# Attention of a two-batch block: score chunks taken ahead of the projection in the heavy steps, and the rest of the step re-ordered to match

## The chip, the cores and the metric

The kernel runs on one core of a Trainium2 chip. The metric is the device time of one execution in microseconds (us), the lower the better. All engines of the core (TensorE or PE, VectorE or DVE, ScalarE or ACT, GpSimd or POOL, and SyncE or SP, which issues all DMAs) run their own instruction lists in order and meet only at semaphores.

## The reference

For 2 batches of 1024 tokens with 512 features it computes `x + s * g`, where `s` is causal attention with ALiBi bias on the layer-normalised input, and `g` the SiLU of a gated feed-forward network.

```python
x = L0_attn_x                       # (2, 1024, 512)
xn = layernorm(x)
q = rmsnorm((xn @ Wq.T) by 32 heads of 128);  k = rmsnorm((xn @ Wk.T) by 8 heads);  v = (xn @ Wv.T) by 8 heads
scores = q @ k.T / sqrt(128) + slope * (key - query)       # -1e30 above the diagonal
s = (softmax(scores) @ v) @ Wo.T
g = silu((silu(xn @ w_gate.T) * (xn @ w_up.T)) @ w_down.T) # inner size 1376
out = x + s * g
```

## The kernel before

Every fp32 operand of a matmul is split in a high half (fp32r) and the rest, and each product is three matmuls (high by high, high by low, low by high). So each tensor that goes to PE is first copied by ACT (`high_...`), and the rest is then made by DVE (`low_...`) or POOL.

The work of a batch is 8 *units*, one for each key/value head with its 4 query heads, and behind them the feed-forward part. A unit is 8 *steps*, one for each tile of 128 queries. Step `i` of unit `U` works on several tiles at once, each engine by a list written out by hand:

- `project` (PE, L365 and L366): q, k and v of tile `i+2`, 24 matmuls. `squares` (ACT) sums their squares, POOL's `norms` makes the reciprocal roots, `scale_qk` (DVE, L751) scales.
- `turn_qk` (PE, L374): transposes of tile `i+1`, then `high_q`, `high_k` (ACT) and `low_q`, `low_k` (DVE, L757, L763). `project` of a tile writes the PSUM accumulator of the tile two before, and so waits until `low_q` and `low_k` of that one are done (`qk_low`).
- `out_project` (PE, L414): the attention output of tile `i-3` by `w_o`, once DVE has scaled it (`scale_att`, L811) and split it (`low_att`, L818). `add_y` (DVE, L827) then empties the PSUM bank `out_ps`.
- `scores` (PE, L388): 4 heads by 1 or 2 *chunks*; tiles 0 to 3 have 1 chunk a head (4 in all), tiles 4 to 7 have 2 (8 in all, up to 512 wide). Chunks go round three PSUM banks, so a chunk waits until DVE's `bias` (L780, which adds the bias, tracks the row minimum and moves the chunk to `probs`) has emptied the bank of three chunks ago.
- `exp` (ACT, L563) of each head, `turn_blocks` (DVE, L791), 32x32 transposes inside the tile, then 16 DMAs issued by SP (`turn_probs`, L273) that bring the blocks home into `pT_lo`, transposed.
- `weigh` (PE, L402): for the tile `p = i-2`, `p+1` blocks of probabilities by v into `out_ps`. Each block needs `high_probs` (ACT, L571) and `low_probs` (DVE, L803); there are four slots for the high halves. The first block also waits for `add_y`.

In step 0 `weigh` works on tile 6 of the unit before, in step 1 on tile 7. In steps 2 to 4 (`LANDS_LATE`) the halves stand later in the lists, since the DMAs land late there. In step 5 ACT and POOL also split the next unit's weights (`high_w`, `low_w`), and in step 2 those of `w_o` (`high_o`, 1.0 us for each of two parts).

PE's list of a step before is `project`, `turn_qk`, `out_project`, all `scores`, `weigh`. What is called a heavy step below is one of 5, 6 and 7.

## Time and profile before

| | us |
|---|---|
| median of 3 runs (lowest, highest) | 2480.33 (2474.41, 2491.34) |
| the profiled execution | 2487.69 |
| its span, first to last instruction | 2485.8 |
| from the start to the end of batch 0's attention, with the start-up | 1028 |
| batch 0's feed-forward part | 236 |

The profiled execution is 7.4 us above the median; 1.9 us of its time lie around the span. The second batch repeats the first. Within a batch the six units between the first and the last are alike; one of them, from 1803.10 to 1929.41 us (its steps 2 to 7 and steps 0 and 1 of the one that follows), is the one that the rows further down look at.

### The profile page before, as it was taken

What the parts mean: (1) busy time and instruction counts of PE and PEld (TensorE: products, weight loads), DVE (VectorE), ACT (ScalarE), POOL (GpSimd) and SP (SyncE); (2) the same over time, 40 slices, a digit from 0 to 9 for tenths busy, and PEclk for the clock granted to TensorE, in tenths of its full rate; (3) what the DMA queues carried; (4) which work ended last, traced back from release to release, by engine and by line L of the source; (5) the groups of instructions that cost most, each with busy time, mean ns of one, the idle gap of its engine ahead of it and who ended that gap; (6) DMA issues with size and microseconds to landing.
All of it is one profiled execution on the core that took longest, in us unless ns stands there. A gap on an engine that the chain in (4) does not pass through costs nothing.

```text
span 2485.8 us, 36949 instructions
## 1 busy us (share of the span) xinstructions
PE 2278.6 (92%) x10928; PEld 1858.0 (75%) x10928; DVE 1794.6 (72%) x3788; ACT 1330.2 (54%) x3700; POOL 826.0 (33%) x2053
## 2 busy tenths in 40 slices
PE   6899989999999999799988999999999999997998
PEld 5777777777777777678877777777777777776887
DVE  5788778787878796831458888888888887887132
ACT  3556555555556565543345565656565556554333
POOL 1424233333332323234514141424242424240443
PEclk8999999999999999999999999999999999999999
DMA  2576857485768585753317766676657766748223
GB/s 91 110 119 97 133 90 135 91 125 103 121 109 119 106 118 102 134 115 124 135 43 129 127 105 107 117 118 114 106 122 102 125 104 114 117 81 158 90 96 108
DMA packets 432681, 277.08 MB, mean 111 GB/s; under 512 B 104672, under 2 KB 399712, under 8 KB 428512
## 3 DMA queue, kind: packets, MB, share of 16 engines
q1 hardware_dynamic: 432480, 274.72, 59.6%
q8 instruction: 87, 1.43, 0.4%
q14 instruction: 114, 0.93, 0.3%
HBM read 119.12 MB, written 4.46 MB: 50 GB/s over the span
## 4 chain that ended last, share of the span: by engine, by line
PE 52%; DVE 20%; issue 7%; SPq 7%; POOL 5%; ACT 4%; DMA 3%; ACTq 0%; DVEq 0%; POOLq 0%
PE out_ps L414 11%; DVE probs L780 9%; PE out_ps L402 9%; SPq L273 7%; PE even_ps L365 5%; PE score_ps L475 5%; PE qkv_ps L365 4%; PE qkv_ps L475 4%; POOL qkv_lo L1032 4%; DVE pT_lo L803 3%; DVE probs L791 3%; PE even_ps L366 3%; PE even_ps L491 2%; PE qkv_ps L366 2%; DMA pT_lo<-probs 2%
## 5 line engine op out<-in xcount | busy, mean ns | idle before, releaser
L563 ACT ACTIVATE probs<-probs,low_min 128x896 f32<-128x896 f32 (+7 forms) x512 | 396.0, 777 | 318.4 <-DVE low_min L780 314.5
L803 DVE TENSOR_TENSOR pT_lo<-pT_lo,pT_hi 128x512 fp32r<-128x512 f32 x576 | 379.0, 693 | 72.3 <-ACT pT_hi L571 71.9
L791 DVE STREAM_TRANSPOSE probs<-probs 128x896 f32<-128x896 f32 (+7 forms) x512 | 382.5, 760 | 0.4
L1002 POOL TENSOR_SCALAR rs_x<-sq_sum 128x5 f32<-128x5 f32 x122 | 24.7, 203 | 1031.2 <-ACT natural L539 1020.6
L571 ACT ACTIVATE pT_hi<-pT_lo 128x512 fp32r<-128x512 f32 x576 | 326.6, 625 | 66.0 <-DMA pT_lo<-probs 47.3
L402 PE MATMUL out_ps<-pT_hi,kv_hi 128*128 128x512 f32 x576 | 247.2, 429 | 97.0 <-DVE pT_lo L803 91.6
L576 ACT ACTIVATE attT_hi<-att 128x512 fp32r<-128x512 f32 x128 | 80.9, 632 | 325.1 <-DVE att L811 325.1
L402 PEld LDWEIGHTS out_ps<-pT_hi,kv_hi 128*128 128x128 f32 x576 | 110.9, 193 | 169.6 <-DVE pT_lo L803 107.9
L402 PE MATMUL out_ps<-pT_lo,kv_hi 128*128 128x512 f32 x576 | 231.5, 402 | 0.0
L402 PE MATMUL out_ps<-pT_hi,kv_lo 128*128 128x512 f32 x576 | 231.2, 401 | 0.0
L388 PE MATMUL score_ps<-kv_hi,qT_hi 128*128 128x384 f32 (+5 forms) x512 | 189.6, 370 | 44.6 <-DVE low_min L780 38.8
L414 PE MATMUL out_ps<-o_hi,attT_hi 128*128 128x512 f32 x512 | 214.0, 418 | 10.7 <-DVE attT_lo L818 10.7
L780 DVE CUSTOM_DVE_ANT_0 probs<-score_ps,rel_sb,slope 128x384 f32<-128x384 f32 (+5 forms) x352 | 202.2, 581 | 6.2 <-DMA pT_lo<-probs 2.4
L414 PE MATMUL out_ps<-o_hi,attT_lo 128*128 128x512 f32 x512 | 203.3, 397 | 0.0
L414 PE MATMUL out_ps<-o_lo,attT_hi 128*128 128x512 f32 x512 | 201.9, 394 | 0.0
L1032 POOL TENSOR_TENSOR qkv_lo<-qkv_raw,qkv_hi 128x768 fp32r<-128x768 f32 x63 | 115.0, 1847 | 194.1 <-ACT qkv_hi L586 181.7
L388 PE MATMUL score_ps<-kv_hi,qT_lo 128*128 128x384 f32 (+5 forms) x512 | 175.4, 342 | 0.0
L388 PE MATMUL score_ps<-kv_lo,qT_hi 128*128 128x384 f32 (+5 forms) x512 | 175.1, 342 | 0.0
L827 DVE TENSOR_TENSOR y<-out_ps,y 128x512 f32<-128x512 f32 x118 | 81.5, 691 | 127.2 <-PE out_ps L414 125.7
L388 PEld LDWEIGHTS score_ps<-kv_hi,qT_hi 128*128 128x128 f32 x512 | 96.8, 189 | 93.6 <-DVE low_min L780 75.1
L1051 POOL TENSOR_TENSOR kv_lo<-qkv_raw,kv_hi 128x1024 fp32r<-128x1024 f32 x44 | 106.4, 2418 | 123.9 <-ACT kv_hi L608 123.9
L402 PEld LDWEIGHTS out_ps<-pT_hi,kv_lo 128*128 128x128 f32 x576 | 111.7, 194 | 25.6
(201 smaller groups left out, 6165.6 us busy)
## 6 DMA issues: line engine op xcount, KB each, us to landing
qkv_raw<-w_ffn_dram SPq DMA_DIRECT2D x44, 768.0 KB, 4.3
att<-rec_out_at SPq DMA_DIRECT2D x128, 256.0 KB
pT_lo<-probs SPq DMA_DIRECT2D x256, 128.0 KB
pT_lo<-probs SPq DMA_DIRECT2D x256, 112.0 KB
pT_lo<-probs SPq DMA_DIRECT2D x256, 96.0 KB
qkv_raw<-w_qkv_dram SPq DMA_DIRECT2D x15, 1536.0 KB
pT_lo<-probs SPq DMA_DIRECT2D x256, 80.0 KB
o_raw<-w_o_dram SPq DMA_DIRECT2D x16, 1024.0 KB, 7.6
```

Source lines behind the costliest of these rows:

```text
L273: sp.dma_start(homes[b * SQUARE:(b + 1) * SQUARE, :, a], by_chunk[i % 2][a * SQUARE:(a + 1) * SQUARE, 0:i + 1, b]).then_inc(probs_back[t % ...
L365: pe.matmul(acc[:, 0:BANK], a, w[:, c, 0:D], start=go, stop=end)
L388: mm = pe.matmul(score_all[n % SBANKS][:, 0:hi - lo], q[:, i % 2, h * P:(h + 1) * P], kt[:, lo:hi], start=(q is qT_hi and kt is kT_hi), st ...
L402: mm = pe.matmul(out_ps[:, :], v[:, j * P:(j + 1) * P], pt, start=(j == 0 and v is v_hi and pt is high), stop=(j == i and v is v_lo))
L414: mm = pe.matmul(out_ps[:, :], a[:, h * P:(h + 1) * P], w[:, h * D:(h + 1) * D], start=(h == 0 and a is attT_hi and w is o_hi), stop=(h == ...
L475: mm = pe.matmul(acc, w[slot][:, at:at + P], xT[:, d, half * BANK:(half + 1) * BANK], start=(d == 0 and w is gu_hi and xT is xT_hi), stop= ...
L563: act.activation(row, row, ACT.Exp, scale=-1.0, bias=low_min[:, i % 2, h, HEAD_CHUNKS[i] - 1:HEAD_CHUNKS[i]], accum_out=row_sum[:, i % 2, ...
L571: act.activation(pT_hi[:, n % HIGH_SLOTS, :], home(i, j).bitcast(F32), ACT.Copy).then_inc(probs_high, 1)
L780: dve.tensor_tensor_reduce(out=by_head[i % 2][:, h, lo // SQUARE:hi // SQUARE, :], in0=score_all[n % SBANKS][:, 0:hi - lo].rearrange("p (m ...
L791: dve.transpose(row, row).then_inc(probs_turned, 1)
L803: dve.tensor_tensor(out=home(i, j), in0=home(i, j).bitcast(F32), in1=pT_hi[:, n % HIGH_SLOTS, :].bitcast(F32), op=ALU.subtract).then_inc(p ...
L1032: pool.tensor_tensor(out=qkv_lo[:, c, :], in0=qkv_raw[:, c, :], in1=qkv_hi[:, c, :].bitcast(F32), op=ALU.subtract).then_inc(w_split if U e ...
```

## The change

A function `parts_of` says how many chunks of a step PE makes ahead of `project` and how many between `project` and `turn_qk`. In the first unit of a batch it says none. In steps 0 to 4 of the other units three stand between `project` and `turn_qk`, and the rest behind `out_project`; in steps 5 to 7 three stand ahead of `project`, three between it and `turn_qk`, and two behind `out_project`. DVE's biases and ACT's exponentials follow this: in heavy steps DVE makes the first three biases ahead of its first four `low_probs`, three more behind them, and the transpose of head 0 ahead of `low_q`; ACT makes head 0's exponential ahead of `squares`, and `high_q`, `high_k` behind `stage_v`. The remaining `low_probs` of a heavy step stand right behind the last bias, ahead of the transposes of heads 1 to 3, and not between them. `low_k` of the next unit's tile 0 (step 7) moves from behind the last bias to behind the transposes of heads 1 and 2. In step 2 `high_o` moves from ahead of `high_probs` to behind three exponentials. In step 5 two of the four `high_w` stand ahead of `high_q`, two behind it.

The rest changes nothing that runs: the slot of a high half is now counted through all units (36 turns in a unit are a multiple of the 4 slots, so that the numbers are the same), `stats` lies in `att[1]`, and the scratch for dynamic DMAs is 256 bytes and not 1024.

```diff
+        def parts_of(i, first):
+            chunks = G * HEAD_CHUNKS[i] if i < TILES else 0
+            if first or not chunks:
+                return 0, 0, chunks
+            return (SBANKS, 2 * SBANKS, chunks) if i > HT else (0, SBANKS, chunks)
...
             def step(U, i, first, last):            # PE
+                ahead, between, chunks = parts_of(i, first)
+                for k in range(ahead):
+                    scores(U, i, k, first)
                 if not (last and i >= TILES - 2):
                     project(U + (i + 2) // TILES, (i + 2) % TILES, first and i + 2 < TILES)
+                for k in range(ahead, between):
+                    scores(U, i, k, first)
                 if not (last and i >= TILES - 1):
                     turn_qk(U + (i + 1) // TILES, (i + 1) % TILES, first and i + 1 < TILES)
...
-                for k in range(sooner):
-                    scores(U, i, k, first)
                 if not (first and i <= LAG):
                     out_project(U, i)
-                for k in range(sooner, chunks):
+                for k in range(between, chunks):
                     scores(U, i, k, first)
...
+                    for h in heads[:ahead // 2]:    # ACT
+                        exp(U, i, h)
+                    heads = heads[ahead // 2:]
...
+                    for h in heads[:-1]:
+                        exp(U, i, h)
+                    if i == LAG:
+                        high_o(U, 0, not first)
+                        high_o(U, 1, not first)
+                    if ahead:
+                        for j in highs:
                             high_probs(V, p, j)
-                        highs = highs[1:]
-                        exp(U, i, G - 1)
...
+                    for k in range(ahead):          # DVE, behind low_att
+                        bias(U, i, k)
...
+                    for k in range(ahead, between): # behind the first four low_probs
+                        bias(U, i, k)
+                    for h in heads[:ahead // 2]:
+                        turn_blocks(U, i, h)
...
-                    if i == TILES - 1 and not last:
-                        low_k(U + 1, 0, False)
...
+                    if ahead:
+                        for j in lows:
+                            low_probs(V, p, j)
+                        lows = []
+                    for h in heads:
+                        for j in lows[:1]:
+                            low_probs(V, p, j)
+                        lows = lows[1:]
+                        if h == G - 1:
+                            if i == TILES - 1 and not last:
+                                low_k(U + 1, 0, False)
+                            reciprocals(U, i)
+                        turn_blocks(U, i, h)
...
-    nc = bacc.Bacc("TRN2", target_bir_lowering=False, num_devices=1, dynamic_dma_scratch_size=1024)
+    nc = bacc.Bacc("TRN2", target_bir_lowering=False, num_devices=1, dynamic_dma_scratch_size=256)
```

**The head of step 7.** On PE, in the fourth unit, the list before from the last matmul of `weigh` (L402) on:

```order
L402 MATMUL out_ps<-pT_hi,kv_lo 128x512
L365 MATMUL qkv_ps<-qkv_hi,xT_hi 128x512
L366 MATMUL qkv_ps<-qkv_hi,xT_hi 128x256
L365 MATMUL qkv_ps<-qkv_lo,xT_hi 128x512
L366 MATMUL qkv_ps<-qkv_lo,xT_hi 128x256
L365 MATMUL qkv_ps<-qkv_hi,xT_lo 128x512
L366 MATMUL qkv_ps<-qkv_hi,xT_lo 128x256
```

and now (L410 is `weigh`, L396 `scores`, L373 and L374 are `project`):

```order
L410 MATMUL out_ps<-pT_hi,kv_lo 128x512
L396 MATMUL score_ps<-kv_hi,qT_hi 128x512
L396 MATMUL score_ps<-kv_lo,qT_hi 128x512
L396 MATMUL score_ps<-kv_hi,qT_lo 128x512
L396 MATMUL third_ps<-kv_hi,qT_hi 128x512
L396 MATMUL third_ps<-kv_lo,qT_hi 128x512
L396 MATMUL third_ps<-kv_hi,qT_lo 128x512
L396 MATMUL score_ps<-kv_hi,qT_hi 128x512
L396 MATMUL score_ps<-kv_lo,qT_hi 128x512
L396 MATMUL score_ps<-kv_hi,qT_lo 128x512
L373 MATMUL qkv_ps<-qkv_hi,xT_hi 128x512
```

Three chunks have come between the last weighing and the projection. On DVE at the same place, before (L811 `scale_att`, L751 `scale_qk`, L818 `low_att`, L803 `low_probs`, L757 `low_q`, L827 `add_y`, L780 a bias with its read of the minimum):

```order
L811 TENSOR_TENSOR att<-out_ps,att 128x512
L751 TENSOR_TENSOR natural<-even_ps,rq 128x640
L818 TENSOR_TENSOR attT_lo<-att,attT_hi 128x512
L803 TENSOR_TENSOR pT_lo<-pT_lo,pT_hi 128x512 x4
L757 TENSOR_TENSOR qT_lo<-even_ps,qT_hi 128x512
L827 TENSOR_TENSOR y<-out_ps,y 128x512
L780 ISA probs,low_min<-score_ps,rel_sb,slope 128x16x32
L780 ISA low_min 128x1
```

and now (the same functions are L837, L777, L844, L829, L783, L853 and L806):

```order
L837 TENSOR_TENSOR att<-out_ps,att 128x512
L777 TENSOR_TENSOR natural<-even_ps,rq 128x640
L844 TENSOR_TENSOR attT_lo<-att,attT_hi 128x512
L806 ISA probs,low_min<-score_ps,rel_sb,slope 128x16x32
L806 ISA low_min 128x1
L806 ISA probs,low_min<-third_ps,rel_sb,low_min,slope 128x16x32
L806 ISA low_min 128x1
L806 ISA probs,low_min<-score_ps,rel_sb,slope 128x16x32
L806 ISA low_min 128x1
L829 TENSOR_TENSOR pT_lo<-pT_lo,pT_hi 128x512 x4
L806 ISA probs,low_min<-score_ps,rel_sb,low_min,slope 128x16x32
L806 ISA low_min 128x1
```

Three biases stand ahead of the four `low_probs`, and `low_q` and `add_y` come later than these rows.

**The end of step 7 on DVE,** from the last bias on, before (L791 `turn_blocks`, L763 `low_k` of the next unit's tile 0, L798 `reciprocals`):

```order
L780 ISA probs,low_min<-third_ps,rel_sb,low_min,slope 128x16x32
L780 ISA low_min 128x1
L791 STREAM_TRANSPOSE probs<-probs 128x32x32
L763 SCALAR_TENSOR_TENSOR kv_lo<-even_ps,wcol,kv_hi 128x128
L803 TENSOR_TENSOR pT_lo<-pT_lo,pT_hi 128x512
L791 STREAM_TRANSPOSE probs<-probs 128x32x32
L803 TENSOR_TENSOR pT_lo<-pT_lo,pT_hi 128x512
L798 RECIPROCAL rec<-row_sum 128x4
L791 STREAM_TRANSPOSE probs<-probs 128x32x32
```

and now (L817, L789 and L824):

```order
L806 ISA probs,low_min<-third_ps,rel_sb,low_min,slope 128x16x32
L806 ISA low_min 128x1
L829 TENSOR_TENSOR pT_lo<-pT_lo,pT_hi 128x512 x2
L817 STREAM_TRANSPOSE probs<-probs 128x32x32 x2
L789 SCALAR_TENSOR_TENSOR kv_lo<-even_ps,wcol,kv_hi 128x128
L824 RECIPROCAL rec<-row_sum 128x4
L817 STREAM_TRANSPOSE probs<-probs 128x32x32
```

Both `low_probs` have moved ahead of all three transposes, and `low_k` from ahead of two of them to behind two.

**Step 2 on ACT,** from `high_att` (L576) on, before (L550 `high_q`, L556 `high_k`, L539 `squares`, L546 `stage_v`, L583 `high_o`, L571 `high_probs`, L563 `exp`):

```order
L576 ACTIVATE attT_hi<-att 128x512
L550 ACTIVATE qT_hi<-qkv_ps 128x512
L556 ACTIVATE kv_hi<-qkv_ps,wcol 128x128
L539 ACTIVATE natural,sq_sum<-even_ps 128x128 x5
L546 ACTIVATE v_nat<-even_ps 128x128
L583 ACTIVATE o_hi<-o_raw 128x1024 x2
L571 ACTIVATE pT_hi<-pT_lo 128x512
L563 ACTIVATE probs,row_sum<-probs,low_min 128x12x32 x4
```

and now (L585, L548, L555, L559, L565, L580, L572 and L592):

```order
L585 ACTIVATE attT_hi<-att 128x512
L548 ACTIVATE natural,sq_sum<-even_ps 128x128 x5
L555 ACTIVATE v_nat<-even_ps 128x128
L559 ACTIVATE qT_hi<-qkv_ps 128x512
L565 ACTIVATE kv_hi<-qkv_ps,wcol 128x128
L580 ACTIVATE pT_hi<-pT_lo 128x512
L572 ACTIVATE probs,row_sum<-probs,low_min 128x12x32 x3
L592 ACTIVATE o_hi<-o_raw 128x1024 x2
L572 ACTIVATE probs,row_sum<-probs,low_min 128x12x32
```

The one `high_probs` of this step no longer stands behind `high_o`.

## Rows read from the trace of the kernel before

**Rows 1.** The page: busy us of each engine, share of the span, instructions.

```profile
PE 2278.6 (92%) x10928; PEld 1858.0 (75%) x10928; DVE 1794.6 (72%) x3788; ACT 1330.2 (54%) x3700; POOL 826.0 (33%) x2053
```

**Rows 2.** Steps 5, 6, 7, 0, 1, 2, 3, 4, then all: us; busy PE, PEld, DVE, ACT, POOL (instructions); clock; DMA.

```profile
1843.23:1858.19 14.96, 14.96 (x78) 12.68 (x77) 14.43 (x32) 11.96 (x31) 5.68 (x13) 1.00 0.71 121
1858.19:1877.03 18.84, 16.93 (x82) 13.37 (x80) 18.13 (x34) 10.56 (x29) 8.80 (x22) 1.00 0.78 161
1877.03:1898.55 21.52, 19.14 (x85) 14.80 (x83) 19.10 (x36) 11.04 (x28) 3.23 (x15) 0.92 0.77 98
1898.55:1914.14 15.59, 15.49 (x75) 12.99 (x74) 10.18 (x26) 8.36 (x29) 3.72 (x15) 0.89 1.09 136
1914.14:1929.41 15.27, 15.13 (x79) 12.27 (x78) 11.89 (x27) 9.31 (x30) 3.22 (x15) 1.00 0.22 49
1803.10:1815.11 12.01, 10.62 (x58) 9.05 (x57) 6.48 (x14) 7.02 (x22) 3.99 (x14) 1.00 0.45 144
1815.11:1827.80 12.69, 12.15 (x61) 9.70 (x60) 10.07 (x23) 7.40 (x26) 8.92 (x19) 1.00 0.32 73
1827.80:1843.23 15.43, 14.28 (x75) 11.66 (x74) 12.84 (x33) 8.21 (x26) 4.59 (x15) 1.00 0.39 89
1803.10:1929.41 126.31, 118.70 (x582) 96.53 (x581) 103.12 (x220) 73.84 (x218) 42.16 (x126) 0.97 0.62 110
```

**Rows 3.** The waits of PE: in total, times, longest.

```profile
PE out_ps L402 <- DVE pT_lo L803: 91.6, 89, 2.6
```

**Rows 4.** DVE in order of time, steps 5 to 7: start, us, what, [idle before].

```profile
1845.27 0.65 DVE L811 TENSOR_TENSOR att<-out_ps,att 128x512 f32<-128x512 f32 x1
...
1867.18 0.69 DVE L827 TENSOR_TENSOR y<-out_ps,y 128x512 f32<-128x512 f32 x1 [0.54 <-PE out_ps L414]
...
1884.70 0.69 DVE L827 TENSOR_TENSOR y<-out_ps,y 128x512 f32<-128x512 f32 x1 [1.49 <-PE out_ps L414]
1885.49 0.75 DVE L780 CUSTOM_DVE_ANT_0 probs<-score_ps,rel_sb,slope 128x512 f32<-128x512 f32 x1
...
1890.08 1.24 DVE L791 STREAM_TRANSPOSE probs<-probs 128x1024 f32<-128x1024 f32 x1
...
1898.79 0.69 DVE L811 TENSOR_TENSOR att<-out_ps,att 128x512 f32<-128x512 f32 x1 [0.52 <-PE out_ps L402]
```

**Rows 5.** PE in order of time, step 7 and the start of step 0.

```profile
1877.03 0.40 PE L365 MATMUL qkv_ps<-qkv_hi,xT_hi 128*128 128x512 f32 x1
...
1884.50 0.39 PE L388 MATMUL score_ps<-kv_hi,qT_hi 128*128 128x512 f32 x1
1884.73 0.39 PE L388 MATMUL score_ps<-kv_lo,qT_hi 128*128 128x512 f32 x1
...
1895.38 0.79 PE L402 MATMUL out_ps<-pT_hi,kv_hi 128*128 128x512 f32 x1 [2.29 <-DVE pT_lo L803]
...
1898.55 0.63 PE L365 MATMUL even_ps<-qkv_hi,xT_hi 128*128 128x512 f32 x1
```

**Rows 6.** The window of 4 us at the end of step 7 (columns as in rows 2).

```profile
1896.00:1900.00 4.00, 3.92 (x11) 2.73 (x10) 3.48 (x6) 0.48 (x1) 0.00 (x0) 0.50 0.06 1
```

**Rows 7.** PE in order of time, end of step 2: first block weighed.

```profile
1814.34 0.47 PE L402 MATMUL out_ps<-pT_hi,kv_hi 128*128 128x512 f32 x1 [1.39 <-DVE pT_lo L803]
```

**Rows 8.** SP issues the 16 DMAs of tile 7, in two units: start, us until all are issued.

```profile
925.71 14.02 SPq L273 DMA_DIRECT2D pT_lo<-probs  x16
...
1898.85 12.95 SPq L273 DMA_DIRECT2D pT_lo<-probs  x16
```

**Rows 9.** ACT takes tile 7's first blocks, in the same two units.

```profile
947.08 2.19 ACT L571 ACTIVATE pT_hi<-pT_lo 128x512 fp32r<-128x512 f32 x4 [6.27 <-DMA pT_lo<-probs]
...
1916.07 2.20 ACT L571 ACTIVATE pT_hi<-pT_lo 128x512 fp32r<-128x512 f32 x4 [0.37 <-DMA pT_lo<-probs]
```

**Rows 10.** Step 1 of the first of these two units (columns as in rows 2).

```profile
939.26:959.71 20.45, 16.27 (x79) 13.57 (x77) 11.97 (x27) 9.63 (x30) 3.66 (x15) 0.92 0.50 138
```

**Rows 11.** The DMA queue of nearly all bytes: packets, MB, share of 16 engines.

```profile
q1 hardware_dynamic: 432480, 274.72, 59.6%
```

82 lines of the change are left out of this document (40 added, 42 removed).

## The prediction

> **What bounds the kernel now.** I read the page first [rows 1]: PE is busy for 2278.6 us, 92% of the span, and DVE for 1794.6. Matmuls overlap in these records (0.39 us each, while the next starts 0.23 us later [rows 5]), so busy time says little of what PE could save. What counts is how long a step lasts against PE's own work in it. The table by steps [rows 2] shows the steady unit: 126.31 us for eight steps. PE's work in a step: projection, turn and output projection take 7.47 us together (1877.03 to 1884.50 [rows 5]); each 512 columns of scores or weighing take 0.23 us, three times a chunk or block, narrower chunks in proportion. That gives, for steps 5, 6, 7: 7.47 + 8 x 0.52 + 4 x 0.69 = 14.4; 7.47 + 8 x 0.60 + 5 x 0.69 = 15.7; 7.47 + 8 x 0.69 + 6 x 0.69 = 17.1. They last 14.96, 18.84 and 21.52. So some 8 us of a unit are lost in these steps. DVE's busy time in steps 6 and 7 is 18.13 of 18.84 and 19.10 of 21.52 [rows 2]: there DVE sets the pace, not PE, and PE's longest wait in total is for `low_probs` (91.6 us in 89 waits [rows 3]).
>
> DVE in order of time [rows 4] shows why DVE itself isn't full. `add_y` waits for PE, which has projection and output projection ahead of it: 1.49 us in step 7, 0.54 in step 6. Only behind it may the biases start (1885.49, 8.5 us into the step), and all eight come in one run with the transposes. So the last two `low_probs` are late, PE idles for 2.29 us before the fifth block [rows 5], and DVE then waits 0.52 us for PE. PE's clock falls with it: the granted clock is 0.50 in the last window, the lower of its two levels (1.2 GHz), and 0.92 and 0.89 over steps 7 and 0 [rows 2, 6].
>
> **The heavy steps.** The change removes no instruction and adds none; it gives DVE three biases at the head of the step, while PE projects. From `scale_att` of step 5 to that of step 0 DVE takes 1898.79 - 1845.27 = 53.52 us, of which three waits are 0.54 + 1.49 + 0.52 = 2.55 [rows 4]: 51.0 of work and small gaps. A bias of 512 costs 0.77 (1885.49 to 1890.08 for six [rows 4]), so in step 7 DVE does `scale_att`, `scale_qk`, `low_att` (2 us), three biases (2.3), four `low_probs` (2.4), and is at 8.4 us when PE has made chunks 3 to 5 (2.1 + 4.2 + 2.1 = 8.4). Three biases and a transpose more and it is at 11.9, `low_q` 12.5, and PE has ended the output projection at 11.6. So `add_y` no longer waits for PE; PE waits for it, until 13.1 (0.3 us after its last chunk). The last two biases end at 14.6, both `low_probs` at 15.8, before PE comes to blocks 5 and 6 at 15.9. PE ends the step at 17.3 and the 2.29 us are gone.
>
> What is late next is `low_k` of the next unit's tile 0. The projection of step 0 writes the accumulator that it reads, so PE waits for it. In DVE's list it now stands behind two more transposes of 1.24 us [rows 4]: 15.8 + 2.3 + 0.3 = 18.4. That is a new wait of 1.1 us in each unit, with PE's whole next projection queued behind it. DVE still has the reciprocals and one transpose to do, 1.3 us.
>
> So steps 5 to 7 last as long as DVE's work: it enters step 5 some 1.6 us behind PE (2.0 before, 1845.27 against the step's start), works 51.0, and releases PE 1.3 before its end: 1.6 + 51.0 - 1.3 = 51.3, against 55.32 before. **Gain 4.0.** Bounds: nothing, if other waits take the place of the three; 7 if DVE's small gaps close too and its backlog is pushed on into step 0, which has room (10.18 busy of 15.59 [rows 2]). The weight split of step 5 (`high_w`, then POOL) starts 1.5 us later with the projection, but the next projection starts 1.8 us later too: no change.
>
> **The clock.** Without the idle PE at the end of step 7 the granted clock should stay at 1.00; step 0 would be 0.89 x 15.59 = 13.9. I take 14.1, **gain 1.5.** The Trainium skill (TensorE: Matmul & The Clock Gate, What's actually happening) says that the low clock is the default and activity lifts it, and so any idle stretch could bring the fall. By that rule the wait for `low_k` may keep the fall, and some 18 us of the total with it; the row shows the fall only behind the 2.29 us wait.
>
> **Step 1 loses.** Tile 7's blocks come home by 16 DMAs that SP issues once all is transposed. The issue takes 13 to 14 us [rows 8], and ACT's first copy came 1916.07 - 1898.85 = 17.2 us after the first issue [rows 8, 9], in step 1. Now the last transpose ends 1.3 us into step 0, the issue starts 0.6 later, and the blocks are there at 1.9 + 17.2 = 19.1, which is 5.0 us into step 1 (1.9 before). ACT's list has `squares`, `high_q` and all exponentials behind that copy. In the unit where the blocks came 7.8 us into step 1 (947.08 against 939.26) ACT sat idle for 6.27 us and the step lasted 20.45 [rows 9, 10], 12.6 us beyond the landing. The three biases now stand in front of `low_q` and chunks are made earlier, which I put at 0.6 us less: 5.0 + 12.0 = 17.0 against 15.27. **Loss 1.7**; bounds: no loss if the DMAs are quicker in a less dense stretch, 6 if all land as late as in that unit (21.4 us after the issue).
>
> **The light steps.** In step 2 PE waits 1.39 us before its only block [rows 7], because ACT's `high_probs` stands behind two `high_o` of 1.0 us each; now it is ahead of them. What stands behind `high_o` is POOL's `low_o` and, behind that, `out_project` of step 3; its second half ends later by about as much as `high_o` does, 0.5 us by my placing of the exponentials, and three chunks now stand in front of `out_project`, 2 us, so it should still be in time. **Gain 1.3** (0 to 1.4). Step 3: PE's work is 7.47 + 4 x 0.69 + 2 x 0.69 = 11.6 of 12.69. Three biases done before `add_y` leave one behind it, and both low halves are ready: **gain 0.9** (0 to 1.1). Step 4: work 7.47 + 8 x 0.44 + 3 x 0.69 = 13.1 of 15.43; the five biases behind `add_y` still pace PE, **gain 1.4** (0 to 2.3). All of these move DVE's work into stretches where it idled; behind them stands only DVE's lag of some 2 us at a step's start, which the projection hides.
>
> **The sum.** 4.0 + 1.5 - 1.7 + 1.3 + 0.9 + 1.4 = 7.4 us in a steady unit. There are 12: 89 us. The two last units have the light steps' gain and the output projection's wait of step 7 hidden by chunks made ahead, but are bound by DVE in steps 6 and 7: 5 us each. The two first have no chunks ahead; their low halves stand in front of the transposes: 2 us each. Together 103 us. The feed-forward part doesn't change. The profiled execution of 2487.69 would take 2385; it lies 7.4 above the median, so 2377, and I say 2375.
>
> **The rivals.**
> - DMA lateness eats more (0.20). If tile 7 lands 21.4 us after the issue in each unit, step 1 lasts 4.2 us more: gain 3.2 a unit, 12 x 3.2 + 14 = 52, 2428. For it: SP's issue and the DMA engines are already dense in step 0 (share 1.09 [rows 2]), and steps get shorter while SP's work of a tile stays at 13 us or more. Against: one unit alone shows it.
> - The heavy steps gain nothing (0.08): the waits for `low_k`, for `add_y` behind `low_q`, and for slots of high halves eat the 4.0. Then 3.4 a unit, 2425.
> - More than forecast (0.17): DVE's small gaps close, step 1 isn't late: 10.5 a unit in all 14 units that change, 147 us, 2333. PE's own work would still allow it.
> - Slower (0.02): the issue of the DMAs gets slower with the scratch cut to a quarter. SP needs about 1.7 us around the 16 DMAs of each of 8 tiles; at 12.95/16 = 0.81 us a DMA [rows 8] that is 8 x 14.6 = 117 us a unit. From 0.90 us a DMA SP alone would pace a unit at 128.8 and the kernel would be over 1% slower; at 1.0 us it is 142 a unit, 2480 + 14 x 15.3 = 2694. Against: the queue is `hardware_dynamic` [rows 11]. The Trainium skill (DMA: Bandwidth & Descriptors, SWDGE vs HWDGE vs iDMA) says that the ring in SBUF serves DMAs issued from GpSimd, and that those from SP have none; by that rule the cut costs nothing, and no run here shows it yet.
> - No difference (0.03): every place that gains is paid back by SP's pace, 14.6 a tile with stalls a little longer than now, 0.88 us a DMA: 2470.
>
> **How the numbers follow.** The forecast has 0.50, with its own range 2350 to 2405. The range of 8 in 10 takes in a good part of the larger gain and of the DMA rival: 2330 to 2430. A measurement of this kernel can tell 1%, 25 us, from no change. Faster by more: 0.50 + 0.20 + 0.08 + 0.17 = 0.95; same 0.03; slower 0.02.
>
> **What would show it.** In the changed profile a steady unit should last about 119 us; step 7 about 18.4, with a wait of the first projection matmul of step 0 for `low_k` of some 1 us in place of the 2.29 us before the fifth block; the granted clock at 1.00 there; ACT's first copy in step 1 waiting some 3 to 4 us for the DMA in most units; no wait in step 2. Wrong would be: `add_y` still waiting for PE in heavy steps; step 1 under 16 us; SP's issue longer than 14 us for a tile.

## The result, and the profile after

The changed kernel takes **2419.7 us** (median of 4 runs, 2408.71 to 2429.22) against 2482.76 us for the kernel before in the same job (4 runs). The ratio is 0.9744, with a 95% interval of 0.969 to 0.9799. The profiled execution takes 2429.22 us, its span is 2427.3, so it is 58.5 us under the span of 2485.8 before. It is the slowest of the four runs: the numbers of waits and steps below are of one execution, and another of the same kernel can differ, as after_again shows further down.

The page's busy time of each engine, to be held against [rows 1]; behind it the page's chain of work that ended last, by engine:

```profile
PE 2231.9 (92%) x10928; PEld 1859.3 (77%) x10928; DVE 1797.2 (74%) x3788; ACT 1332.8 (55%) x3700; POOL 812.3 (33%) x2053
PE 50%; SPq 19%; DVE 10%; issue 8%; DMA 5%; POOL 4%; ACT 4%; ACTq 0%; DVEq 0%; POOLq 0%
```

The instructions are the same in number. DVE had 20% of the chain before and SP's queue 7%; now DVE has 10% and SP's queue 19%. The change took much of DVE's work off the path, and what came onto it is the issue of DMAs.

The table by steps shows where: steps 5, 6, 7, 0, 1, 2, 3, 4 and their sum, of the stretch of the second batch that begins nearest to the one of [rows 2] (columns as there):

```profile
1804.66:1820.39 15.73, 14.68 (x79) 12.84 (x77) 15.41 (x34) 11.71 (x31) 5.39 (x11) 1.00 0.81 117
1820.39:1836.65 16.26, 16.17 (x81) 13.68 (x80) 15.74 (x33) 9.98 (x27) 9.21 (x24) 1.00 1.13 177
1836.65:1855.51 18.86, 17.49 (x85) 14.05 (x83) 18.48 (x36) 11.04 (x28) 3.52 (x15) 1.00 0.96 132
1855.51:1870.01 14.50, 13.95 (x75) 11.92 (x76) 11.02 (x28) 8.58 (x29) 3.23 (x15) 1.00 0.71 100
1870.01:1888.25 18.24, 16.45 (x79) 13.49 (x77) 11.79 (x27) 9.61 (x30) 3.28 (x15) 0.91 0.41 89
1888.25:1899.15 10.90, 10.59 (x57) 9.07 (x56) 6.90 (x16) 6.64 (x23) 3.25 (x14) 1.00 0.53 168
1899.15:1911.12 11.97, 11.82 (x60) 9.69 (x59) 11.41 (x23) 8.32 (x27) 9.59 (x19) 1.00 0.49 79
1911.12:1925.11 13.99, 13.39 (x75) 11.68 (x74) 12.29 (x31) 8.14 (x26) 4.54 (x15) 1.00 0.71 98
1804.66:1925.11 120.45, 114.54 (x581) 96.41 (x580) 103.04 (x221) 74.02 (x219) 42.00 (x126) 0.99 0.74 120
```

Every step but 1 and 5 is shorter, DVE's busy time is the same (103.04 and 103.12), and the granted clock no longer falls in steps 7 and 0; it falls in step 1 (0.91), which is 3 us longer. The units aren't alike any more. So the numbers below are means over the 12 steady units of a trace; a step is measured from the start of its first matmul to that of the next step's.

| mean of 12 units, us | 0 | 1 | 2 | 3 | 4 | 5 | 6 | 7 | unit |
|---|---|---|---|---|---|---|---|---|---|
| before | 15.44 | 15.56 | 11.99 | 12.69 | 15.46 | 15.17 | 18.93 | 21.36 | 126.59 |
| changed | 14.62 | 17.40 | 10.82 | 12.25 | 15.31 | 15.58 | 16.64 | 19.21 | 121.83 |
| least of the 12, changed | 14.48 | 15.62 | 10.79 | 11.97 | 13.99 | 14.44 | 16.16 | 18.83 | |

The wait of 2.29 us before the fifth block [rows 5] is gone, and a wait of the next projection for `low_k` stands in its place: first PE at the start of step 0 and DVE's `low_k`, then the window of 4 us ahead of it, to be held against [rows 6] (two views of the changed kernel).

```profile
1855.51 0.50 PE L373 MATMUL even_ps<-qkv_hi,xT_hi 128*128 128x512 f32 x1 [1.30 <-DVE kv_lo L789]
...
1855.14 0.31 DVE L789 SCALAR_TENSOR_TENSOR kv_lo<-even_ps,wcol,kv_hi 128x128 fp32r<-128x128 f32 x1
```

```profile
1852.00:1856.00 4.00, 2.69 (x13) 1.95 (x12) 4.00 (x7) 1.60 (x4) 0.00 (x0) 1.00 0.48 114
```

The largest waits of the changed kernel that matter here, from the list of waits (us in total, times, longest):

```profile
ACT pT_hi L580 <- DMA pT_lo<-probs: 80.0, 34, 7.1
...
DVE probs L806 <- DMA pT_lo<-probs: 43.0, 23, 4.7
...
DVE y L853 <- PE out_ps L422: 38.9, 33, 3.4
...
PE even_ps L373 <- DVE kv_lo L789: 18.7, 14, 1.6
...
PE out_ps L410 <- DVE pT_lo L829: 6.3, 6, 1.4
```

PE's wait for `low_probs` fell from 91.6 us [rows 3] to 6.3, and the wait for `low_k` gives back 18.7, 1.3 in each of 14 units. The first two lines are the 16 DMAs of a tile. ACT's `high_probs` waited for them before too, for 47.3 us in 23 waits. The second line is new in this size: before it was 4.2 us in 3 waits; now 27.9 of its 43.0 us lie in step 4. It is `bias`, which may not write `probs` before the DMAs of the tile *two before* have read it, since two `probs` buffers take turns. In step 4 of one unit (DVE and SP in order of time, changed kernel):

```profile
2032.43 0.69 DVE L844 TENSOR_TENSOR attT_lo<-att,attT_hi 128x512 fp32r<-128x512 f32 x1
2036.02 0.55 DVE L806 CUSTOM_DVE_ANT_0 probs<-score_ps,rel_sb,slope 128x320 f32<-128x320 f32 x1 [2.90 <-DMA pT_lo<-probs]
...
2006.96 14.60 SPq L281 DMA_DIRECT2D pT_lo<-probs  x16
2022.93 10.23 SPq L281 DMA_DIRECT2D pT_lo<-probs  x16
```

SP needed 14.60 us for the 16 DMAs of tile 1, so that the 16 of tile 2 were issued by 2033.16 only; the wait for them ended at 2036.0. The first bias of tile 4, which the change had put at the head of the list, waited 2.90 us for them, with `low_q`, `low_k` and all other biases behind it. This step 4 lasted 16.71 us, where the one in the table above lasted 13.99.

### The profile page after: what moved, and what is told of

It is laid out like the page before. It is cut to its first block, busy times and chain, and to the rows that moved or that the text cites. A ratio compares the mean times of both kernels' runs of the same rounds, so it can differ in the third digit from the quotient of the medians.

```text
span 2427.3 us, 36949 instructions
## 1 busy us (share of the span) xinstructions
PE 2231.9 (92%) x10928; PEld 1859.3 (77%) x10928; DVE 1797.2 (74%) x3788; ACT 1332.8 (55%) x3700; POOL 812.3 (33%) x2053
## 4 chain that ended last, share of the span: by engine, by line
PE 50%; SPq 19%; DVE 10%; issue 8%; DMA 5%; POOL 4%; ACT 4%; ACTq 0%; DVEq 0%; POOLq 0%
SPq L281 17%; PE out_ps L410 9%; PE out_ps L422 7%; PE score_ps L396 5%; PE score_ps L484 5%; PE qkv_ps L484 5%; PE qkv_ps L373 3%; PE even_ps L373 3%; DMA pT_lo<-probs 3%; DVE probs L817 3%; DVE probs L806 2%; PE third_ps L396 2%; PE even_ps L500 2%; DVE pT_lo L829 2%; POOL qkv_lo L1067 2%
## 5 line engine op out<-in xcount | busy, mean ns | idle before, releaser
L572 ACT ACTIVATE probs<-probs,low_min 128x896 f32<-128x896 f32 (+7 forms) x512 | 395.6, 784 | 145.7 <-DVE low_min L806 142.5
L829 DVE TENSOR_TENSOR pT_lo<-pT_lo,pT_hi 128x512 fp32r<-128x512 f32 x576 | 374.4, 689 | 135.1 <-ACT pT_hi L580 133.5
L580 ACT ACTIVATE pT_hi<-pT_lo 128x512 fp32r<-128x512 f32 x576 | 331.1, 624 | 179.5 <-PE out_ps L410 93.5
L817 DVE STREAM_TRANSPOSE probs<-probs 128x896 f32<-128x896 f32 (+7 forms) x512 | 372.3, 754 | 0.0
L410 PE MATMUL out_ps<-pT_hi,kv_hi 128*128 128x512 f32 x576 | 243.0, 422 | 66.1 <-issue 46.7
L585 ACT ACTIVATE attT_hi<-att 128x512 fp32r<-128x512 f32 x128 | 81.0, 633 | 346.8 <-DVE att L837 345.5
L806 DVE CUSTOM_DVE_ANT_0 probs<-score_ps,rel_sb,slope 128x384 f32<-128x384 f32 (+5 forms) x352 | 204.3, 591 | 51.5 <-DMA pT_lo<-probs 41.7
L396 PE MATMUL score_ps<-kv_hi,qT_hi 128*128 128x384 f32 (+5 forms) x512 | 180.3, 352 | 60.7 <-DVE low_min L806 57.2
L410 PE MATMUL out_ps<-pT_hi,kv_lo 128*128 128x512 f32 x576 | 231.3, 401 | 0.0
L410 PE MATMUL out_ps<-pT_lo,kv_hi 128*128 128x512 f32 x576 | 231.0, 401 | 0.0
L410 PEld LDWEIGHTS out_ps<-pT_hi,kv_hi 128*128 128x128 f32 x576 | 112.4, 195 | 124.2 <-issue 75.3
L396 PE MATMUL score_ps<-kv_hi,qT_lo 128*128 128x384 f32 (+5 forms) x512 | 175.9, 344 | 0.0
L396 PE MATMUL score_ps<-kv_lo,qT_hi 128*128 128x384 f32 (+5 forms) x512 | 175.6, 343 | 0.0
L396 PEld LDWEIGHTS score_ps<-kv_hi,qT_hi 128*128 128x128 f32 x512 | 97.4, 190 | 88.6 <-DVE low_min L806 72.1
L410 PEld LDWEIGHTS out_ps<-pT_hi,kv_lo 128*128 128x128 f32 x576 | 111.7, 194 | 25.6
L844 DVE TENSOR_TENSOR attT_lo<-att,attT_hi 128x512 fp32r<-128x512 f32 x128 | 124.9, 975 | 5.6 <-ACT attT_hi L585 5.6
```

Of the source, the lines that this page charges most:

```text
L396: mm = pe.matmul(score_all[n % SBANKS][:, 0:hi - lo], q[:, i % 2, h * P:(h + 1) * P], kt[:, lo:hi], start=(q is qT_hi and kt is kT_hi), st ...
L410: mm = pe.matmul(out_ps[:, :], v[:, j * P:(j + 1) * P], pt, start=(j == 0 and v is v_hi and pt is high), stop=(j == i and v is v_lo))
L572: act.activation(row, row, ACT.Exp, scale=-1.0, bias=low_min[:, i % 2, h, HEAD_CHUNKS[i] - 1:HEAD_CHUNKS[i]], accum_out=row_sum[:, i % 2, ...
L580: act.activation(pT_hi[:, (U * TURNS + n) % HIGH_SLOTS, :], home(i, j).bitcast(F32), ACT.Copy).then_inc(probs_high, 1)
L806: dve.tensor_tensor_reduce(out=by_head[i % 2][:, h, lo // SQUARE:hi // SQUARE, :], in0=score_all[n % SBANKS][:, 0:hi - lo].rearrange("p (m ...
L817: dve.transpose(row, row).then_inc(probs_turned, 1)
```

## Experiments

Ratios are against the kernel before on the same chip, with their 95% intervals. The steps are those of one profiled execution of each, and that one can lie off the median: by 9 us in before_half and by 15 in after_again, both below it. The first four ran on one chip (before: 2468.66 us), the next four on another (2472.07), the last four on a third (2472.28). All means of steps are made like those above.

| | us | ratio | unit | step 0 | 1 | 2 | 3 | 4 | 5 to 7 |
|---|---|---|---|---|---|---|---|---|---|
| scratch1024 | 2386.87 | 0.9674 [0.9633, 0.9715] | 118.73 | 14.62 | 16.01 | 10.81 | 12.01 | 14.33 | 50.95 |
| light_only | 2452.18 | 0.9922 [0.989, 0.9954] | 124.22 | 16.04 | 15.57 | 10.83 | 12.13 | 14.66 | 54.99 |
| heavy_only | 2444.39 | 0.9896 [0.9861, 0.9932] | 123.39 | 14.46 | 17.46 | 10.54 | 14.28 | 15.38 | 51.26 |
| low_k_first | 2380.3 | 0.964 [0.9612, 0.9669] | 118.35 | 14.55 | 16.73 | 10.82 | 12.21 | 14.42 | 49.60 |
| after_again | 2392.73 | 0.9665 [0.964, 0.969] | 118.63 | 14.75 | 15.73 | 10.81 | 11.99 | 14.32 | 51.03 |
| scratch_again | 2387.98 | 0.9658 [0.9634, 0.9681] | 119.48 | 14.74 | 16.18 | 10.82 | 12.02 | 14.52 | 51.21 |
| half_issue | 2373.71 | 0.9604 [0.9587, 0.9621] | 118.60 | 14.74 | 15.61 | 10.81 | 12.00 | 14.00 | 51.45 |
| split_issue | 2433.68 | 0.9859 [0.9834, 0.9884] | 121.92 | 16.07 | 15.92 | 10.80 | 12.23 | 14.19 | 52.71 |
| before_half | 2462.47 | 0.9959 [0.9941, 0.9976] | 125.04 | 14.77 | 15.26 | 11.97 | 12.65 | 15.43 | 54.95 |
| half_low_k | 2349.68 | 0.9508 [0.9487, 0.9528] | 116.83 | 14.50 | 15.58 | 10.81 | 12.00 | 14.00 | 49.93 |
| heavy_q_first | 2441.66 | 0.9885 [0.9858, 0.9911] | 123.17 | 14.69 | 16.34 | 10.91 | 14.39 | 16.64 | 50.20 |
| half_blocks | 2380.62 | 0.9629 [0.9605, 0.9652] | 118.95 | 14.77 | 15.61 | 10.82 | 12.15 | 14.63 | 50.98 |

**scratch1024: is it the scratch?** The changed kernel with the scratch of before.

```diff
-dynamic_dma_scratch_size=256
+dynamic_dma_scratch_size=1024
```

> The changed kernel with the scratch for dynamic DMAs back at 1024 bytes, nothing else. Theory A (the scratch serves no DMA of this kernel, and SP's issue is as long as before): as the changed kernel, 2420 us, ratio to before 0.974 within half a per cent, and SP still some 12 us for the 16 DMAs of a tile. Rival B (the smaller scratch slows the issue and is why the DMAs come late): under 2400 us, issue nearer 10.3 us a tile.

It came out well under the changed kernel's result, and under theory B's bound too, but with 11.71 us for the issue of 16 DMAs and not nearer 10.3, and on another chip. So it was run again (scratch_again) beside the changed kernel itself (after_again).

> The changed kernel once more, to stand beside the next three on one chip. Its first comparison gave a ratio to before of 0.9744 [0.969, 0.980] on another chip; with the scratch at 1024 on a later chip the ratio was 0.9674 [0.963, 0.972]. If the scratch is without effect, this one and the next agree within half a per cent.

> The changed kernel with 1024 bytes of scratch, on the same chip as the 256 bytes of the run ahead. Theory A (the scratch does nothing, and chips differ in how fast their DMAs land): the same ratio as the run ahead within 0.5%. Rival B (256 bytes cost something): 0.7% or 17 us less than the run ahead.

Side by side they are 0.9658 and 0.9665, with intervals that overlap: no effect of the scratch is seen. The Trainium skill (DMA: Bandwidth & Descriptors, SWDGE vs HWDGE vs iDMA) gives DMAs issued from SP no ring in SBUF; these two runs agree with it. What the first run had seemed to show is how comparisons differ: the same changed kernel has 0.9744 in the first one and 0.9665 here. The waits tell which part differs between the two traces. Of after_again, the waits for the 16 DMAs:

```profile
ACT pT_hi L580 <- DMA pT_lo<-probs: 30.4, 21, 3.1
...
DVE probs L806 <- DMA pT_lo<-probs: 15.8, 10, 3.3
```

46.2 us instead of 123.0. Step 2 is the same in both and steps 5 to 7 differ by 0.4 us; steps 1 and 4 differ by 1.7 and 1.0 (15.73 and 14.32 against 17.40 and 15.31). But the trace of after_again is of the fastest of its five executions (2377.79, the slowest took 2394.74), the first one of the slowest of four. scratch_again's trace, of an execution of 2394.05 us on the same chip, has 48.9 us of these waits. So part of the difference is between executions on one chip, and how much of it is the chip isn't shown.

**light_only, heavy_only: which part gives what?** `parts_of` alone is changed.

```diff
-            return (SBANKS, 2 * SBANKS, chunks) if i > HT else (0, SBANKS, chunks)
+            return 0, SBANKS, chunks                                                 # light_only
+            return (SBANKS, 2 * SBANKS, chunks) if i > HT else (0, 0, chunks)        # heavy_only
```

> Heavy steps 5 to 7 take three chunks between projection and turn and none ahead of the projection, like the light steps; the rest as changed. Theory A (the heavy steps' chunks ahead are worth 4 us a unit, of which DMA lateness in the steps behind eats some 2): steps 5 to 7 last about 54 to 55 us, step 1 back at 15.3 to 15.6, step 7 again with a wait of PE for the low halves or for add_y: 2440 to 2455 us. Rival C (chunks between projection and turn already feed DVE in time, the ones ahead bring nothing): 2420 us as changed.

> Steps 0 to 4 make no chunk between projection and turn (all four or eight stand behind the output projection, as before); the heavy steps and ACT's and DVE's order as changed. Theory A (light steps gain little in sum, since their early biases only meet the wait for the DMAs that empty the probabilities' buffer, some 1.5 to 2 us a unit come from step 2 alone): 2425 to 2440 us, with hardly a wait of a bias for a DMA in step 4. Rival D (the light steps' chunks are worth the 3.6 us a unit that was forecast for steps 2 to 4): 2460 to 2470 us.

Each alone gives some 1%, both together give 3.3% (scratch1024, same chip). light_only came out as its theory A said; heavy_only is 4 us above its theory A and 16 below rival D. Its other sign of theory A is there: no bias waited for the DMAs at all, so it takes the light steps' early chunks to bring that wait. The steps say why the parts don't add up. Chunks ahead in the heavy steps give 4.2 us in steps 5 to 7 in heavy_only as well (55.46 to 51.26). But in both halves the *lists around the chunks* stay as the change made them, and each has a price if its cover is missing. In light_only `low_k` stands late although no bias of step 7 is ahead of the projection: step 7 lasts 21.83 and the next projection waits for it (19.2 us in 14 waits). The granted clock of the step 0 behind it is 0.87 in one unit (1743.60 to 1759.94), and step 0 lasts 16.04 in the mean. In heavy_only step 3 lasts 14.28 us against 12.69 before, and DVE waits for ACT there.

**heavy_q_first: is it `squares` ahead of `high_q`?** heavy_only, with ACT's order of before in the light steps:

```diff
-                    if first:
+                    if not between:
                         turned()          # high_q, high_k
                     ... squares, stage_v ...
-                    if not first:
+                    if between:
                         turned()
```

> heavy_only (chunks ahead in steps 5 to 7 alone, 2444.39 us on its chip, ratio 0.9896) with one more edit: in steps 0 to 4 ACT makes high_q and high_k ahead of squares and stage_v, as before the change. In heavy_only the steady step 3 takes 14.05 us against 12.69 us before, and DVE waits there for ACT's high_q. Theory A, the two parts of the change help each other since ACT's new order (squares first) needs the chunks between projection and transposes: with high_q first, step 3 is 12.7 us again, step 2 stays under 12.0, and the time falls by 12 x 1.3 = 16 us or somewhat more, to 2425 us, ratio 0.982. Theory B, the order of ACT is nothing, and it is the lateness of the DMAs that makes the sum of the parts less than the whole: step 3 stays near 14 us, 2444 us, ratio 0.990.

No: step 3 stays at 14.39, and 2441.66 us is near theory B's 2444. The order of `high_q` isn't what makes it long; that the lateness of the DMAs does, as theory B went on, isn't seen either, since one wait of a bias for them is left (1.0 us). The list of waits of heavy_q_first and DVE in order of time show another of the moved pieces:

```profile
DVE rec L824 <- ACT probs L572: 22.7, 16, 1.5
```

```profile
1780.34 0.18 DVE L824 RECIPROCAL rec<-row_sum 128x4 f32<-128x4 f32 x1 [1.45 <-ACT probs L572]
```

The last exponential of step 2 now stands behind both `high_o` (1.99 us), and without chunks made ahead DVE has nothing else left and waits 1.45 us for it. heavy_only has the same wait (22.5 us, 16 times); in the changed kernel it is 4.4 us in all. It is of the size of most of the 1.7 us in step 3, but that it is the cause isn't shown: a version with `high_o` alone moved wasn't run. A rival is untested as well. The change also moved the transposes of heads 0 and 1 in the light steps, from between the biases to behind all of them, and this stays in both versions. Where step 4's 16.64 comes from (15.38 in heavy_only) I didn't settle.

**half_issue, before_half: what do the DMAs cost each kernel?** SP issues 8 of the 16 DMAs of a tile; what they would have brought stays zero, so that half of the transposed probabilities are left out. The compute engines do the same work in the same order otherwise, with one more memset by POOL at the start.

```diff
-PER_TURN = BLOCKS * BLOCKS * 16
+PER_TURN = BLOCKS * BLOCKS // 2 * 16
...
-                    for k in range(BLOCKS):
+                    for k in range(BLOCKS // 2):
```

> The changed kernel with 8 of the 16 DMAs that bring a tile's blocks home left out (half of each block's squares stay what they were, so the output is not the reference's), and one memset more at the start. SP's issue and the bytes both halve. Theory A (late DMAs are what the forecast's gain was lost to, 2 to 3 us a unit on average over their floors in steps 1, 3, 4 and 5): no wait of ACT or DVE for these DMAs, steps 1, 3, 4 at their shortest, 15.6, 12.0 and 14.0, unit about 117.5 us, 30 to 50 us below the changed kernel. Rival D (the engines' own order sets the time): at most 10 us below.

> This is the kernel before the change, with 8 of the 16 DMAs of each tile left out (half of the transposed probabilities stay zero, and the waits count 8). It asks what the transfers cost the kernel before, as half_issue (2373.71 us) asked it of the changed one. Theory A, the earlier chunks are what brings the waits for these DMAs to the path: before, only one of the twelve steady units stands above its usual 126.3 us (287.32 to 420.49 us, 133.17 us), so that the transfers cost it some 7 us in all, 2472 - 7 = 2465 us, ratio 0.997. The changed kernel without them would then be 91 us under this one, 7.6 us for each steady unit, and the transfers would account for the rest of what was missing. Theory B, the transfers cost both kernels alike: half_issue was 19 us under the changed kernel on its chip, so 2472 - 19 = 2453 us, ratio 0.992.

The changed kernel gains 19 us on its chip (2392.73 to 2373.71), and no wait of ACT or DVE for these DMAs is left. That is less than the 30 to 50 us of theory A (against the 2419.7 us of the first comparison it would be 46) and more than rival D's 10; steps 1, 3 and 4 are at the lengths theory A named (15.61, 12.00 and 14.00), in all 12 units. The kernel before gains 10 us (2472.28 to 2462.47), near theory A's 7. Between their two traces the unit is 1.55 us shorter, 0.67 of it in step 0. So the kernels differ by 88.8 us without the lateness, by 79 with it on that chip, and by 63 in the first comparison. SP's issue of a tile's 16 takes about as long in both kernels (11.64 us in the mean before, 12.02 and 11.63 in the two traces of the changed one). The kernel before waited for them too, and the changed kernel waits at more places.

**half_blocks: issue or bytes?** All 16 DMAs are issued, each with half of the blocks (again half of the probabilities are left out).

```diff
-    homes[..., :, a],              by_chunk[..., 0:i + 1, b]
+    homes[..., 0:(i + 2) // 2, a], by_chunk[..., 0:(i + 2) // 2, b]
```

> The changed kernel with all 16 DMAs of each tile issued, but each carrying only the first (i+2)/2 of the i+1 blocks, about half the bytes (half of the transposed probabilities stay zero). With half as many DMAs of full size the changed kernel took 2373.71 us, and 2392.73 with all. Theory A, what is late is SP's issue (16 in a row take 11.6 us a tile): it stays late with half the bytes, 2388 us or more. Theory B, it is the bytes in the DMA engines (from the last issue to the landing): 2374 to 2378 us.

2380.62 lies between the two theories, and so does the ratio. Step 1 is as short as in half_issue (15.61), step 4 isn't (14.63). Its waits:

```profile
DVE probs L809 <- DMA pT_lo<-probs: 20.7, 10, 4.5
ACT pT_hi L583 <- DMA pT_lo<-probs: 12.7, 14, 3.2
```

SP's issue of 16 took 11.56 us in the mean of all tiles, and 11.63 in after_again: half the bytes don't shorten the issue. Tile 7 had landed (the last event of its semaphore) 13.0 us after its first issue instead of 16.0, in the mean of its 16 units. So, as far as single executions on two chips can be compared, ACT's wait in step 1 depends on the bytes (1.8 us left of 21.2) and DVE's wait in step 4 on the issue (15.6 us against 13.1). The one follows the largest tile; ahead of the other are two short steps (10.8 and 12.0 us), in which SP, with 10 to 16 us a tile, falls behind.

**split_issue: let ACT issue four of them.** Four of the 16 DMAs of a tile go to ACT's queue, behind `high_att`.

```diff
-                for a in range(BLOCKS):            # SP
+                for a in range(BLOCKS - 1):
...
+                    a = BLOCKS - 1                 # ACT, behind high_att
+                    for k in range(BLOCKS):
+                        act.dma_start(homes[...], by_chunk[...])
```

> The changed kernel with 4 of the 16 DMAs of each tile issued by ACT, behind its copy for the attention output at the head of the next step, and 12 by SP; all that is computed stays. If SP's issue of 16 times 0.65 us is what makes the blocks late (theory A1), they land 2.5 us sooner in the light tiles and most waits of biases for DMAs in steps 3 and 4 go: 10 to 25 us less than the changed kernel. If bytes and engines set the landing (A2), only SP's queue gets shorter: within 5 us. ACT pays 4 issues a step, which delays its high halves by up to 2.5 us: it could cost 10 us and more if ACT's order counts (rival D).

It is worse, by 41 us against after_again, as rival D had it. The lateness did shrink, as theory A1 had it: 13.2 us of ACT's waits for these DMAs are left and none of DVE's, of 46.2. But ACT pays for it. The list of waits, then ACT in order of time at the head of an ordinary step 5:

```profile
ACT pT_hi L580 <- issue: 173.9, 74, 5.5
```

```profile
1800.11 2.58 ACTq L634 DMA_DIRECT2D pT_lo<-probs  x4
1802.79 2.20 ACT L580 ACTIVATE pT_hi<-pT_lo 128x512 fp32r<-128x512 f32 x4 [2.11 <-issue]
```

Four issues hold ACT for 2.62 us as a rule (the median of 128 tiles, from 2.50 up), with `high_probs` behind them and `low_probs` and PE behind those. Against after_again step 0 went from 14.75 to 16.07 in the mean and step 5 from 15.54 to 17.27. The slowest four of all took 5.94 us:

```profile
1851.16 5.94 ACTq L634 DMA_DIRECT2D pT_lo<-probs  x4
1857.20 2.19 ACT L580 ACTIVATE pT_hi<-pT_lo 128x512 fp32r<-128x512 f32 x4 [5.47 <-issue]
```

and the windows of the steps 7 and 0 around it (columns as in rows 2):

```profile
1830.45:1849.33 18.88, 17.52 (x85) 14.05 (x83) 18.50 (x36) 10.81 (x28) 3.23 (x15) 1.00 0.86 112
1849.33:1869.98 20.65, 16.64 (x74) 13.70 (x75) 11.25 (x28) 8.56 (x29) 3.22 (x15) 0.83 0.95 115
```

This step 0 lasted 20.65 us, those of the other steady units 15.4 to 16.4. The Trainium skill (Trainium Kernel Development and Optimization, Key Constraints) says that issuing from several engines only saves the sequencer's issue time. Here that time was what SP lacked. One issue cost ACT as much as SP (0.65 us at 2.62 for four), but on ACT it stood ahead of work that PE waits for.

**low_k_first: the wait for `low_k`.** `low_k` stands ahead of the transposes of step 7, `high_k` ahead of the last exponential.

```diff
                     if i == TILES - 1 and not last:      # ACT
                         high_k(U + 1, 0, False)
                     for h in heads[-1:]:
                         exp(U, i, h)
...
+                    if i == TILES - 1 and not last:      # DVE, behind the last low_probs
+                        low_k(U + 1, 0, False)
                     for h in heads:
...
-                            if i == TILES - 1 and not last:
-                                low_k(U + 1, 0, False)
```

> The changed kernel with low_k of the next unit's tile 0 ahead of the transposes of heads 1 to 3 in step 7, and high_k ahead of the last exponential on ACT, so that PE's first projection of step 0 no longer waits (1.3 us a unit in the changed kernel). Rival D (the engines' own order is what is left to gain): the whole wait comes back, 14 x 1.5 = 20 us less, 2400 us. Theory A (the DMAs of tile 7 set when step 1 can go on): they are issued no earlier, so steps 7 and 0 end 1.5 us sooner and step 1 lasts up to 1.5 us longer in units where tile 7 was late: 2408 to 2416 us.

The time is 2380.3 us, 6.6 under scratch1024 on the same chip, with intervals that meet. The expectations were given in times of the first comparison; theory A's 4 to 12 us less fits and rival D's 20 doesn't. Step 7 is 1.48 us shorter than in scratch1024 (17.40 to 18.88), but step 1 is 0.72 longer: tile 7's blocks come as late as before, and PE is there sooner. In half_low_k both edits are in, and half the probabilities are left out again.

> The changed kernel with low_k of the next unit's tile 0 ahead of the transposes of step 7 and high_k ahead of its last exponential, and with 8 of the 16 DMAs of each tile left out (half of the transposed probabilities stay zero). With all 16, low_k_first took 1.47 us off step 7 and gave 0.7 to 1.0 us of it back in step 1. Theory A, what it gave back is lateness of tile 7's DMAs alone: here step 7 is 17.4 us and step 1 stays at 15.6 us, 12 x 1.45 = 17 us under half_issue, 2356 us (2353 to 2360). Theory B, what low_k and high_k are moved past (the exponential and the transposes of step 7) is itself on the path: step 1 or step 0 grows by 0.7 us or more with half the DMAs as well, 2365 us or more.

2349.68, 24 us under half_issue and so somewhat more than theory A's 17. Step 7 is 17.41, and step 1 stays at 15.58: what low_k_first gave back in step 1 was the DMAs' alone. Windows of steps 7, 0 and 1 in half_low_k, and then in low_k_first:

```profile
1766.80:1784.21 17.41, 17.33 (x84) 14.24 (x83) 17.02 (x33) 11.03 (x28) 3.50 (x15) 1.00 0.61 68
1784.21:1798.72 14.51, 13.87 (x75) 11.72 (x74) 12.50 (x30) 8.44 (x29) 3.21 (x15) 1.00 0.89 85
1798.72:1814.28 15.56, 15.08 (x79) 12.23 (x77) 11.72 (x27) 9.67 (x30) 3.26 (x15) 1.00 0.47 127
```

```profile
1788.17:1805.58 17.41, 17.34 (x85) 14.23 (x83) 17.03 (x33) 11.06 (x28) 3.48 (x15) 1.00 0.94 133
1805.58:1820.07 14.49, 13.87 (x75) 11.73 (x74) 12.48 (x30) 8.47 (x29) 3.20 (x15) 1.00 0.84 90
1820.07:1838.61 18.54, 16.49 (x79) 13.46 (x77) 11.79 (x27) 9.64 (x30) 3.25 (x15) 0.91 0.53 113
```

The same steps 7 and 0 to 0.02 us, and then 3 us of difference in step 1. Of the versions that compute everything, low_k_first has the lowest ratio, 0.964, though its interval meets that of scratch1024.

## Why the prediction was right, and where its sum was off

The direction, the mechanism of the heavy steps and the range held: 2375 us was forecast with 2330 to 2430, 2419.7 was measured. The gain was forecast as 105 us and is 63. Point by point, by the profiled executions:

- **The heavy steps, 4.0 a unit: right.** Steps 5 to 7 went from 55.46 to 51.43 us, 4.0, and from 55.46 to 51.26 in heavy_only. `add_y`'s wait for PE fell from 125.7 us in all to 38.9; in steps 5 to 7 alone it fell from 38.3 us to 1.8. The wait for `low_k` came as forecast, 1.3 us and not 1.1, and low_k_first shows its price: step 7 is 1.48 shorter without it.
- **The clock, 1.5: right in mechanism, half in size.** The granted clock is 1.00 in the last window and in step 0. The prediction allowed for a fall at the wait for `low_k`, from the rule that the low clock is the default and activity lifts it (the Trainium skill, TensorE: Matmul & The Clock Gate, What's actually happening); here 1.30 us of idle PE left it at 1.00. Step 0 went from 15.44 to 14.62, 0.8 (14.5 in every steady unit of the changed kernel but the first, where it is 16.0). How much of it belongs to the change depends on the execution of before: in before_half step 0 lasts 14.0 to 15.5 us, 14.77 in the mean, which is as long as in half_issue (14.74). A step 0 of before at full clock took 14.05 (one of before_half, clock 1.00), and one of the changed kernel takes 14.50: 0.45 us are new, most of them in its narrow chunks, which are now in two pieces.
- **Step 1, loss of 1.7: met in this execution, with luck.** 15.56 to 17.40, 1.8. ACT's first copy in the unit of the table waited 3.60 us for the DMA, within the 3 to 4 foreseen. But the trace is of the slowest execution. In after_again step 1 is 15.73, a loss of 0.2 and under the 16 us that the prediction had named as a sign of being wrong. The mechanism is real, its size is that of the DMAs' lateness, and the prediction had taken that from two tiles.
- **Step 2, 1.3: right** (1.2). **Step 3, 0.9: half.** 0.4 in the mean, 0.7 in the least.
- **Step 4, 1.4: this is the term of a steady unit that failed.** The mean fell by 0.15 us. The least, 13.99, is 1.5 under before, and in half_issue all twelve are at 14.00. The price of the compute was right; the prediction had counted the DMAs' lateness for one reader only, ACT in step 1, and wrote of steps 2 to 4 that behind them "stands only DVE's lag". The bias of the tile two later waits for the same 16 DMAs, for its buffer; in the list of before the biases come later, and waited for them 4.2 us in all.
- **The last units, 5 each: right; the first units, 2 each: wrong in sign.** All of the span outside the 12 steady units took 966.7 us before and 965.4 in the changed kernel. From one execution of the changed kernel to the next this part moves by about as much as the forecast 14: 952.4 in after_again, 958.5 in scratch_again. With the lateness out of the way it is 951.4 (before_half) and 948.7 (half_issue), 2.7 us less and not 14. Steps 3 to 7 of the first unit and all of the last unit of a batch, batch 0, in before_half and then in half_issue (columns as in rows 2):

```profile
72.31:156.16 83.85, 77.03 (x374) 62.07 (x373) 75.52 (x152) 48.78 (x136) 31.40 (x83) 0.99 0.58 72
906.84:1056.96 150.12, 131.47 (x610) 105.26 (x608) 116.45 (x239) 81.15 (x213) 42.58 (x104) 0.95 0.59 88
```

```profile
75.57:161.69 86.12, 76.59 (x374) 61.60 (x372) 75.37 (x153) 49.78 (x138) 31.80 (x83) 1.00 0.54 70
873.28:1018.50 145.22, 126.94 (x609) 104.40 (x610) 118.61 (x240) 81.97 (x213) 41.26 (x104) 0.98 0.58 91
```

  The last unit is 4.9 us shorter (5.1 in batch 1), the first 2.3 us longer (3.0). The first unit has the lists around the chunks without the chunks. Its step 7 lasts 22.3 us in both kernels that have the new lists, half_issue and the changed one, and 20.9 to 21.5 in the two that have the old ones; that it is `low_k`, as in light_only, wasn't tried there.
- **The other signs of being wrong.** An issue of over 14 us was to be one. 14 of the 128 tiles took longer, up to 16.54, but 7 of 128 did before too, up to 16.75, and the mean is 12.02 us against 11.64. The prediction had read 12.95 and 14.02 us from two tiles and taken 12.95 for all, so its 117 us a unit for SP before was too high.

The sum: 12 x (7.4 - 4.76) = 32 us are missing in the steady units and 12.6 outside them, of 103 - 58.5 = 44.5. Of the 2.64 us a unit, step 4 has 1.25, step 0 0.7, step 3 0.5. By the time alone the rival that the heavy steps gain nothing (2425) was nearest and the one of late DMAs (2428) next, but steps 5 to 7 rule out the first. The second had put everything into step 1, at 21.4 us after the issue in each unit; step 1 lost no more than the forecast had, and what came on top stood in step 4. half_issue shows what the lateness costs: without it the changed kernel is 19 us faster by the medians, the kernel before 10, and the difference between the two grows from 79 to 89 us. By the traces the steady unit of half_issue is 6.4 us under that of before_half (118.60 and 125.04) and 8.0 under that of before; the trace of before_half is 9 us under its median, so the first number is rather low. Why the issue of 16 DMAs takes 10.1 us in one tile and up to 16.5 in another stays open, and so does why a kernel's executions differ in it.

## What to carry to other kernels

When work is moved ahead, look for every wait that the moved instruction has, those on buffers too (who must have *read* this buffer?), and ask how much slack each of them had under the old order; a wait that never showed is not one that costs nothing. An order that belongs to a change (here a late `low_k`) is only as good as the work that covers it, so halves of a change measured alone can hide most of its worth, and a part of the kernel that takes the new order without the new work can lose. And once the compute engines are off the path, count what the DMA-issuing queue needs for a round of the loop: here some 12 us a tile against steps of 10.8 and 12.0. And before a term is called right or wrong by one trace, look where its execution lies among the others.
